# Attention's slot on TensorE: the output projection moved between two products of the projection of x

## The reference

```python
x = x + 0.5 * ffn(layernorm(x))                 # 64 experts, the best 8 for each token
qkv = layernorm(x) @ w_qkv.T                    # 16 heads of 64
q, k, v = split(qkv)
q = q * cos + rotate_half(q) * sin + fenc
k = k * cos + rotate_half(k) * sin + fenc
attn = softmax(q @ k.T * 64 ** -0.5)
x = x + (attn @ v) @ w_out.T + b_out
x = x + 0.5 * ffn(layernorm(x))
```

## Time and profile before

| | us |
|---|---|
| three timed runs | 917.76, 916.82, 915.58 (median 916.82) |
| span of the profiled execution, first to last instruction | 912.4 |
| of that, attention: first scores to the second mixture's first DMA | 293.1 to 662.2 |
| PE busy over the span | 845.9 (93%) |
| DVE, ACT, POOL busy | 568.7, 503.1, 492.2 |

### The profile page before, as it was taken

How to read it: one execution, slowest core, us unless ns; L and a number is a source line. 1 busy time by engine, 2 the same in 40 slices (tenths; PEclk the granted TensorE clock), 3 DMA queues, 4 the chain that set the end, 5 groups by cost and what they waited for, 6 DMA issues and landing times.

```text
span 912.4 us, 18887 instructions
## 1 busy us (share of the span) xinstructions
PE 845.9 (93%) x6360; PEld 748.5 (82%) x6360; DVE 568.7 (62%) x1738; ACT 503.1 (55%) x1376; POOL 492.2 (54%) x536
## 2 busy tenths in 40 slices
PE   5989989999964899999999999999879999999968
PEld 4889989999963677777777777777679999999954
DVE  8947753333336877788888888877543385333337
ACT  4422333333322888888888888888732333333327
POOL 4156777777752222256666666666557254444440
PEclk9779999999996999999999999999999999999989
DMA  9947877777626890000000000000050688888648
GB/s 321 374 160 226 255 232 225 235 237 228 202 90 224 197 151 1 1 17 28 22 25 22 28 22 25 22 20 14 6 211 18 218 299 285 279 289 280 228 134 316
DMA packets 68479, 140.72 MB, mean 154 GB/s; under 512 B 10479, under 2 KB 37552, under 8 KB 68292
## 3 DMA queue, kind: packets, MB, share of 16 engines
q1 hardware_dynamic: 56644, 118.59, 40.0%
q0 software_dynamic: 11776, 21.39, 7.6%
HBM read 107.72 MB, written 35.56 MB: 157 GB/s over the span
## 4 chain that ended last, share of the span: by engine, by line
PE 51%; POOL 11%; ACT 11%; DVE 9%; issue 7%; DMA 4%; SPq 0%; DVEq 0%; ACTq 0%; POOLq 0%
PE ps L1370 12%; ACT at_prob L2255 7%; PE ps L615 7%; PE ps L1949 6%; PE ps L1389 6%; POOL y_rows L589 5%; POOL f_xg L578 5%; DVE at_nmax L2078 3%; PE ps L72 3%; PE ps L1990 2%; PE ps L655 2%; DMA f_yt<-y_rows 2%; PE ps L1975 2%; PE ps L1962 2%; ACT at_qkT L2249 2%
## 5 line engine op out<-in xcount | busy, mean ns | idle before, releaser
L1843 POOL TENSOR_TENSOR at_m<-at_m 128x512 f32<-128x512 f32 x64 | 81.4, 1272 | 146.4 <-DVE at_m L2071 146.4
L1181 POOL DMA_INDIRECT xs_rows<-xr,slots_of x128 | 127.2, 994 | 43.6 <-issue 32.0
L2255 ACT ACTIVATE at_prob<-ps,at_nmax 128x256 f32<-128x256 f32 x256 | 117.8, 474 | 39.5 <-DVE at_nmax L2078 39.0
L1350 POOL DMA_INDIRECT y_rows<-f_og,f_put x80 | 80.0, 1001 | 97.8 <-ACT f_og L1502 78.0
L878 DVE TENSOR_TENSOR f_ehid<-f_esil,ps 128x480 f32<-128x480 f32 (+1 forms) x80 | 50.7, 634 | 116.1 <-ACT f_esil L719 107.8
L1639 DVE TENSOR_TENSOR f_hid<-f_sil,ps 128x480 f32<-128x480 f32 (+1 forms) x80 | 50.6, 634 | 106.4 <-ACT f_sil L1495 99.8
L1370 PE MATMUL ps<-f_xgT,f_ring 128*128 128x160 f32 x768 | 115.0, 299 | 1.7 <-issue 1.7
L615 PE MATMUL ps<-f_xgT,f_ring 128*128 128x160 f32 x768 | 114.9, 299 | 0.2 <-issue 0.2
L719 ACT ACTIVATE f_esil<-ps 128x480 f32<-128x480 f32 (+1 forms) x80 | 44.3, 554 | 120.9 <-PE ps L615 120.9
L1495 ACT ACTIVATE f_sil<-ps 128x480 f32<-128x480 f32 (+1 forms) x80 | 44.3, 554 | 120.3 <-PE ps L1370 120.3
L1370 PEld LDWEIGHTS ps<-f_xgT,f_ring 128*128 128x128 f32 x768 | 107.0, 190 | 2.1 <-issue 2.1
(11 more groups left out here) (256 smaller groups left out, 1847.6 us busy)
## 6 DMA issues: line engine op xcount, KB each, us to landing
f_ring<-in_wexp SPq DMA_DIRECT2D x128, 576.0 KB, 5.0
y_rows<-zeros SPq DMA_DIRECT2D x16, 512.0 KB, 6.1
f_yt<-y_rows SPq DMA_DIRECT2D x16, 512.0 KB, 8.9
at_yt<-y_rows SPq DMA_DIRECT2D x6, 1024.0 KB, 4.9
xs_rows<-at_blank SPq DMA_DIRECT2D x16, 342.5 KB, 10.2
f_xg<-xs_rows SPq DMA_DIRECT2D x16, 342.5 KB, 3.4
y_rows<-f_og,f_put POOLq DMA_INDIRECT x160
y<-y_rows SPq DMA_DIRECT2D x4, 512.0 KB, 4.4
```

Source lines behind the costliest of these rows:

```text
L1181: nc.gpsimd.indirect_dma_start(xs_dram, bass.IndirectOffsetOnAxis(s.slots_of[:, t, k:k + 1], 0), s.xr[:, t, :], None, bounds_check=last_sl ...
L1843: nc.gpsimd.tensor_tensor(m1[:, p % 2, :], m1[:, p % 2, :], m2[:, p % 2, :], ALU.add).then_inc(msum, 1)
L2255: mm = nc.scalar.activation(prob[:, p % 2, h, t, :], ps[:, SB + h, t * SEQ:(t + 1) * SEQ], ACT.Exp, bias=nmax[:, p % 2, h, t:t + 1], accum ...
```

## The change

In `qkv` the part for the values' rows becomes a function of its own, `v_rows`, which `batch` calls after `project`. So the slot's end, which was *q/k products, v products, projection*, becomes *q/k products, projection, v products*. Since the `oev` wait of the v products no longer stands ahead of `project`, `project` has a wait of its own for the `take_o` a slot earlier, everywhere. The number of matmuls, and the programs of the four other engines, stay as they are.

```diff
                     mm.then_inc(qk, 1)
+
+                def v_rows(b, p, xs):
+                    u = PAIRS * b + p
                     taken = u - AHEAD - VLAG + 1
...
-                def project(b, p, more, alone=True):
+                def project(b, p, more):
                     u = PAIRS * b + p
-                    if alone:
-                        pe.wait_ge(oev, u + 1)
+                    pe.wait_ge(oev, u + 1)
...
                         if there(b, p, JLAG, first, last):
-                            project(*earlier(b, p, JLAG), not last, last and p + AHEAD >= PAIRS)
+                            project(*earlier(b, p, JLAG), not last)
+                        if p + AHEAD < PAIRS:
+                            v_rows(b, p + AHEAD, xcur)
+                        elif not last:
+                            v_rows(b + 1, p + AHEAD - PAIRS, xnext)
                         if p == LN_TURN and not last:
                             turn_x(b + 1, False)
```

More of the change, by code:

```diff
@@ L2043, in _ @@
                 qkv(0, 0, xnext)
+                v_rows(0, 0, xnext)
                 qkv(0, 1, xnext)
+                v_rows(0, 1, xnext)
                 turn(0, 0)
                 qkv(0, 2, xnext)
+                v_rows(0, 2, xnext)
                 pe.wait_ge(xc, 1)
```

## The result

Over four runs each, the changed kernel takes 909.8 us (909.23 to 910.41) and the kernel before 916.2 us (915.35 to 917.76). The ratio is 0.9939, with a 95% interval of 0.9919 to 0.9959: **faster, by 3.8 to 7.4 us**. The forecast was 911.8 us and faster.

A forecast was written before the change was run, and what follows sets the result against it. No engine alone bounds attention; TensorE's and ScalarE's mutual waits do. Gains of 3.4 us outside batches 2 to 5 and 1.6 in them make 5.0, taking 916.82 to 911.8 us; range 909.5 to 917.5, the forecast's own 910.0 to 914.5.

The forecast's parts named there:

- The wait at the v products: TensorE's v products waiting for `take_o`, 12.0 us in all: gone with 0.14 us to spare, except where VectorE is late.
- The step from the v products to the scores: New TensorE step from the last v product's start to the scores: 0.21 us, giving ordinary slots of 5.29 instead of 5.62.
- the dear price of 0.30: Upper price for the step from v products to scores, 0.30 us instead of 0.21; total gain then 2.9 us.
- rival (3): Slower: drain ahead of the 64-row scores behind a 256-column product; at a 0.60 us step, 920.4 us; chance 0.12.
- rival (2): TensorE's new steps eat the gain: 0.10 us excess on each of two, 4.4 of 5.0 us, 916.2; chance 0.22.
- The wait at `values`: `values` waits for ScalarE's `take_v` in about every second ordinary slot, up to 0.3 us; two slots take 10.88 us.
- The new wait: The projection's own wait for `take_o` of the slot before: finished over 5 us earlier, so it costs nothing.
- What comes after attention: Work behind attention's barrier, at 662.22 us with the weights' DMAs: a gain in attention passes on in full.
- The sum: Ordinary slots outside batches 2 to 5 give 3.4 us and four loop batches 1.6: together 5.0 us.
- the term of 0.18 for each ordinary slot: Gain per ordinary slot outside batches 2 to 5 after the `take_v` loop: 0.18 us, over 20 slots 3.6 us.
- the 0.2 taken off where runs break off: Deduction of 0.2 us from 3.6 where runs of ordinary slots break off at a routing slot, leaving 3.4.
- the loop term: Batches 2 to 5: 0.39 us each, 0.33 from slots 1 to 3 and 0.06 from ordinary-routing pairs; 1.6 us together.

The follow-up runs named there:

- after_early_v: The changed kernel with `take_v` moved ahead of the second `normalise` on ScalarE: 902.99 us, ratio to the kernel before 0.9862.
- before_wait: The kernel before, with the projection given its own wait for `take_o` of a slot earlier but keeping its place: 916.05 us, ratio 0.9997.

## Why the prediction was right

**The wait at the v products** fell as worked out. The projection's last record starts at about 352.28 + 0.335 = 352.615; the v products follow at 352.64, their successor 0.20 later. The prediction carried 0.02 and 0.20 over from the end of `turn_p`, and nothing extra was paid. The row of 12.0 us is gone. Where VectorE is late (slot p = 2 of the loop batches) a short delay is left that has no row in the waits: in batch 3 the v products start 0.54 behind the projection's start instead of 0.36, which is the remainder that the prediction allowed for.

```profile
443.08 0.61 PE L1992 MATMUL ps<-wout,at_oTh 128*128 128x128 f32 x4
443.62 0.38 PE L72 MATMUL ps<-wqkv_high,at_xcur 128*128 128x256 f32 x1
```

**The step from the v products to the scores**, the term without a row of its own, was taken at 0.21 and is 353.17 - 352.96 = 0.21. So the dear price of 0.30, the drain of rival (3) and the excess of rival (2) are out. The v product's record is 0.28 long, and the scores start 0.07 before it ends. Nor was 0.30 a dearer price: in the trace before, the records of the scores start in pairs 0.21 apart, so the step from the last pair to `values` (0.31) is 0.10 beyond their own spacing, just as the projection's 0.205 is 0.09 beyond its 0.11. The rule of the Trainium skill, page "TensorEngine Tiling (Array Packing)", section "Tiling Modes", that a change of mode drains TensorE, can show here at most in the 0.09 us by which the new step exceeds the products' own spacing of 0.12 us, not in a whole record.

**The wait at `values`** takes back what the prediction said. The loop over two slots was put at 10.88 us and measures 5.31 + 5.57 = 10.88. That `take_v` is the cause, and not TensorE's steps, was only argued there; after_early_v shows it, since with `take_v` earlier the second slot falls to 5.29 too.

**The new wait** costs nothing (before_wait). **What comes after attention** keeps its distance: the DMA of the earlier trace rows starts at 658.57 in the changed kernel instead of 662.22, as much earlier as the last slot's scores (646.11 instead of 649.77). From those scores to that DMA it is 12.45 or 12.46 us in all twelve profiles, so the gain passes on in full. From the DMA to the end of the span the profiles differ by themselves, 249.2 to 251.4 us; that it is nearly the same before and after (250.2 and 250.1) is partly chance.

**The sum** was 5.0 us and attention shows 5.35. That it comes so close is in part luck, since its two parts miss in opposite directions (slot 0 of batch 2 is counted with batches 0 and 1, slot 0 of batch 6 with the loop batches):

| | predicted | measured |
|---|---|---|
| batches 0, 1, 6, 7 | 3.4 | 1.72 (0 and 1) + 1.45 (6 and 7) = 3.17 |
| loop batches 2 to 5 | 4 x 0.39 = 1.6 | 0.41 + 0.40 + 0.55 + 0.81 = 2.17 |

Outside the loop, the term of 0.18 for each ordinary slot holds wherever the slots stand in a run (16 slots give 3.06). What was too small is the 0.2 taken off where runs break off: the four ordinary slots next to a routing slot give only about 0.1 together, not 0.5. In batches 2 and 3 the loop term is right to 0.02: slots 1 to 3 give 0.35 (0.33 was put down), slots 4 and 5 0.05 (0.03), slots 7 and 0 nothing (0.03). The step that was mis-sized is that these stood for all four. The prediction read batch 3 only, and in batches 4 and 5 VectorE made more slots late before: slots 4 and 5 took 11.51 there instead of 11.35, and slots 1 to 3 of batch 5 17.62 instead of 17.36. After, that delay is not seen: the four batches are alike in slots 4 and 5 (11.30 to 11.31), and batches 3 to 5 in slots 1 to 3 (17.01). Which slots are late varies between executions: in before_wait slots 4 and 5 take 11.34 to 11.36 in all four batches, and slots 1 to 3 17.63 and 17.58 in batches 4 and 5. Measured from that profile the loop term is 2.11, so it is above 1.6 there too; what makes VectorE late in one execution and not in another stays open.

**From the sum to the median.** The forecast was 911.8 us and the median is 909.8: inside the range of 909.5 to 917.5, but 0.2 below the forecast's own range of 910.0 to 914.5. Of the 2.0 us between them, 0.6 come from the median before, which is 916.2 with a fourth run where the forecast started from 916.82, and 0.35 from the sum. The remaining 1.05 is not explained by the mechanism. It is less than what the start of attention moves by itself from run to run (2.3 us among the twelve profiles), and the 95% interval of 3.8 to 7.4 us holds both the 5.0 forecast and the 6.4 measured.

The 4.4 us between the profiled span and the median before can now be divided. In all four runs of the changed kernel the time is only 1.7 to 1.8 us above its own span (910.41 with a span of 908.7). With that, the profiled execution of before took about 912.4 + 1.7 = 914.1, an estimate, below each of the four timed ones: most of the 4.4 was difference between executions. The forecast did not suffer, since it kept the 4.4 on both sides.

## What to carry to other kernels

When work is moved into the gap of one wait, look at the next wait of that queue which was just met before: of the gain, whatever exceeds its slack is held there in that round (here 0.03 us of slack against 0.33 of gain). Over a loop of two slots the part that remains can be worked out ahead from one slot's rows, since each late start also puts off the next round of the engine that is waited for. And an edit that is worth nothing alone may be worth more than the change itself once the change is in: `take_v` earlier gave 0 before and 336.49 - 330.24 = 6.25 us after.

## What the runs showed of the hardware that I had not expected

The half clock (1.2 GHz) ahead of attention lasts a different time from run to run. In both kernels PE runs nothing from 270 to 282 us, the granted clock falls meanwhile (0.63 and 0.62 over 270 to 275, 0.50 over 275 to 280), and PE then works at the half clock with nearly the same busy time (1.9 of 2 us from 286 to 288, 1.3 from 288 to 290, then without a gap). It rises to 2.4 GHz within 290 to 292 us before (granted 0.56 in that stretch, 1.00 in the next), and only within 294 to 296 us after (0.50 in the two stretches ahead of it, 0.74 there). The 1.69 us by which attention starts later in the profile are a third of the effect that was to be measured.
